# Eight batches through a staged front and six local attention layers: the front's order rewritten around its gathers, gated values in three pieces

## The chip, the cores and the metric

The kernel runs on one core of one Trainium2 chip. The metric is the device time of one execution in microseconds. An execution of the kernel before was also profiled; all rows of traces come from that one.

## The reference

Inputs are eight batches of 256 tokens of 256 numbers, token indices into small tables, and a few condition vectors for each batch. With everything in float32:

```python
# condition block
h = ln(x, pw_g[pathway], pw_b[pathway]); h = ln(h, cp_g[comp], cp_b[comp])
t = ln(x, tm_g[time], tm_b[time]);       s = ln(x, ms_g[scale], ms_b[scale])
m, n, r = (x + mlp_ln(state_k)[:, None, :] for the three condition vectors)
cat = concat([w[0]*h, w[1]*t, w[2]*m, w[3]*n, w[4]*r, w[5]*s])   # w = softmax(aw)
y = mlp_ln(cat)
# 16-head attention on y; its scale comes from maxima and norms of q, k and y
x = x + attention(y)
# modulated linear, attention of each token's 16 heads on one another, modulated linear
o = modulated_linear(heads(modulated_linear(x, cond_512)), cond_512)
# six layers on z, which starts as o; every sublayer first shifts half the features by one token
for i in range(6):
    z = local_attention(shift(z), Wqkv[i], rotary, window=64) @ Wo[i] + z
    a, gate = split(ln(shift(z)) @ W1[i] + b1[i])
    z = (a * gelu(gate)) @ W2[i] + b2[i] + z
out = x + z
```

## The kernel before

`build` (L2240) first lets GpSimd write the identity matrix and zero `state` (128 partitions x 4112 numbers: all eight batches, transposed, each with a column of padding ahead of each half), and then has a barrier of all engines. Three stages follow, each ended by a barrier: `front`, `local_layers` and `write_out`.

**Front** (L153). One batch after another runs through the condition block, the attention in eight pairs of heads, and the attention of each token's heads. Every engine has a list of its own. A helper table says at which step `t` which operation runs for which batch: `for q in batches(t, 60): gather(q)` issues batch q's gather at step 60 + 8q, and where several operations share a step the order of the loops decides. The numbers set nothing but the order within one engine; between the engines semaphores decide. The operations that the steps of the prediction touch:

- SyncE (`sp`) loads inputs at the start: indices, x, the small nets' inputs and first weights (`s_t`, `m_w1`), biases `fcols`, their second weights `m_w2`, the mixer's weights `w_int`, `aff`, and the attention's weights. Twelve of these signal one semaphore, `net`.
- GpSimd (`pool`, L240): `gather` (L263) copies the indices and issues six indirect DMAs (L273), two for each of three tables, into `pw`, `ct` and `ms`. `scale_h`, `scale_t`, `scale_s` and `affine_h` (L282 to L310) multiply by the gathered rows and add them, two instructions each. `net_root` (L255), `dem_root` (L259), `root` (x, h, y) and `scale_root` (L312, writes `scl`) are inverse roots. `head_out` (L324, eight a batch, writes `prodo`) multiplies scores by values of the heads, and `turn_k` writes `kd`.
- TensorE (`pe`): `net_hidden` (L401, its matmuls L405), `net_out` (L413), `style_mm` (L437) and `dem_mm` (L447) for the small nets; `net_flip`, `net_bias` (L430); transposes of x, t, s and h (recorded as L398); `mixer_hidden` (L488); later `scale_row`, whose transposes (L560) bring the score scale into rows.
- ScalarE takes the mixer's hidden values (`hid_t`, L782). VectorE normalises, takes `scol` (L1168) from `scl`, makes the products `prod` (L1237) and the sums `o` of `prodo` (L1267).

Two PSUM banks, `bank_m0` and `bank_m1`, pass between many operations in a fixed cycle (tables `BANK0`, `BANK1`).

**Layers** (L1410). Six layers by eight batches make 48 passes of eight units. A unit projects four heads of q, k or v (`project`, L1598, in high and low halves of the numbers), turns them by the rotary tables, flips them (`flip_qk`: TensorE L1623, ScalarE's copy `qk_t` L1819), scores, softens and flips the probabilities (`prob_t`, L1838), and applies them to the values (`attend`; ScalarE's copy `attn_hi`, L1846). Then come W_o, the layer norm, and W1 in six tiles (NJ = 6), whose second half goes through the GELU. `gelu`, `gate_value`, `hidden_hi` and `hidden_lo` treat the six tiles in two parts of three, and `w_2_mm` waits before tiles 0 and 3. Weights come through one buffer, `w_raw`, in pieces; for the first piece of the first layer (L1517) SyncE issues the load after those of `rot_cos`, `rot_sin`, `band` and two layers' `cols` and `qk_gain`, and VectorE splits it (`split_wqkv`, L1972 and L1974) and then x (L2008, L2010), before TensorE can start.

## Time and profile before

| | |
|---|---|
| median of 3 executions | 3338.82 us (3336.04 to 3339.55) |
| the profiled execution, its own time | 3341.73 us |
| span of its trace | 3340.3 us |
| busy shares: TensorE, VectorE, ScalarE, GpSimd | 92%, 79%, 76%, 62% |
| mean granted clock of TensorE | 0.964 of full speed |
| start to the first batch's hidden values | 0 to 76.6 us |
| batches of the front | 76.6 to 649 us |
| layers | 649 to about 3331 us |

Busy shares are means over stages that differ. The rows below show each engine in short stretches: a timeline row has the start, the duration, the engine and line, output and inputs with their shapes, and in brackets how long the engine was idle before the instruction and which instruction of which engine (or which DMA) ended that.

### The profile page before, as it was taken

The page shows a single profiled execution, that of the slowest core. Times are in us where ns is not written, and L with a number is a line of the kernel's source. Part 1 is how long each engine was busy: PE and PEld are TensorE (multiplying, and loading weights), DVE is VectorE, ACT ScalarE, POOL GpSimd, SP SyncE. Part 2 cuts the span into 40 slices and gives each one's busy share as a digit, 9 for nine tenths or more (in the row PEclk, how much of TensorE's full clock was granted, in tenths as well). Part 3 has the DMA queues.
Part 4 walks back from the last instruction along what each step waited for, and adds up shares of the span by engine and source line. Part 5 has one row for each costly group of instructions (what it writes and reads, how often), then busy time and mean ns, then how long its engine had stood idle before and what let it go on. Part 6 is the DMA issues. An engine that isn't in the chain of part 4 may idle for free. (4 is left out here: it accounts for less than half of the span.)

```text
span 3340.3 us, 80712 instructions
## 1 busy us (share of the span) xinstructions
PE 3079.5 (92%) x29936; PEld 2725.4 (82%) x29936; DVE 2639.1 (79%) x5117; ACT 2535.9 (76%) x7059; POOL 2074.1 (62%) x1536
## 2 busy tenths in 40 slices
PE   3888797279999999999999999999999999999997
PEld 3666565168999899998999989999899998999996
DVE  2368789678888988889887898888888878888884
ACT  0687677168878787878887878878788878888884
POOL 4446654466666666666666667666666666666662
PEclk8898898599999999999999999999999999999999
DMA  3111100010000100001100010000100000100000
GB/s 122 57 36 32 61 7 4 29 41 29 2 2 11 42 30 1 2 2 36 44 3 1 2 36 25 21 2 2 30 23 30 2 2 13 40 29 8 5 8 26
DMA packets 27780, 75.04 MB, mean 22 GB/s; under 512 B 4120, under 2 KB 9848, under 8 KB 27256
## 3 DMA queue, kind: packets, MB, share of 16 engines
q1 hardware_dynamic: 22224, 52.63, 5.0%
q0 software_dynamic: 4864, 16.78, 1.6%
q8 instruction: 242, 3.96, 0.5%
q14 instruction: 146, 1.20, 0.1%
q10 hardware_dynamic: 304, 0.47, 0.1%
HBM read 65.68 MB, written 4.19 MB: 21 GB/s over the span
## 5 line engine op out<-in xcount | busy, mean ns | idle before, releaser
L1571 POOL TENSOR_TENSOR turned<-by_cos,turned 128x512 f32<-128x512 f32 x384 | 493.2, 1284 | 853.6 <-DVE turned L2026 853.5
L1575 POOL TENSOR_TENSOR rnorm<-norm,half 128x8 f32<-128x8 f32 x384 | 788.2, 2053 | 0.0
L1829 ACT ACTIVATE prob<-ps_s,ebias,rnorm 128x128 f32<-128x128 f32 x1536 | 682.0, 457 | 62.5 <-DVE ebias L2047 61.8
L2040 DVE TENSOR_REDUCE negmax<-ps_s 128x8 f32<-128x1024 f32 x192 | 235.1, 1225 | 291.2 <-PE ps_s L1652 290.8
L1838 ACT ACTIVATE prob_t<-ps_t 128x512 f32<-128x512 f32 x384 | 230.0, 599 | 226.6 <-PE ps_t L1661 222.1
L2055 DVE TENSOR_TENSOR prob<-prob,rinv 128x512 f32<-128x512 f32 x384 | 374.9, 976 | 13.1
L1598 PE MATMUL ps_qk<-w_hi,x_hi 128*128 128x512 f32 x768 | 336.9, 439 | 25.1 <-DVE x_lo L2010 14.2
L1737 PE MATMUL ps_f<-hid_hi,w_hi 128*128 128x256 f32 (+1 forms) x1056 | 308.3, 292 | 5.7 <-DVE hid_lo L2101 5.6
L1829 ACT ACTIVATION_READ_ACCUMULATOR prob<-ps_s,ebias,rnorm 128x1 f32 x1536 | 311.6, 203 | 0.0
L1598 PE MATMUL ps_qk<-w_lo,x_hi 128*128 128x512 f32 x768 | 305.2, 397 | 0.0
L1598 PE MATMUL ps_qk<-w_hi,x_lo 128*128 128x512 f32 x768 | 304.9, 397 | 0.0
L2020 DVE TENSOR_TENSOR by_cos<-ps_qk,cos_t 128x512 f32<-128x512 f32 x384 | 265.4, 691 | 44.8 <-ACT sq L1802 42.3
L1737 PE MATMUL ps_f<-hid_hi,w_lo 128*128 128x256 f32 (+1 forms) x1056 | 297.4, 282 | 0.0
L1737 PE MATMUL ps_f<-hid_lo,w_hi 128*128 128x256 f32 (+1 forms) x1056 | 297.2, 281 | 0.0
L1578 POOL TENSOR_TENSOR turned<-turned,rnorm 128x256 f32<-128x256 f32 x384 | 275.6, 718 | 30.1
L1802 ACT ACTIVATE sq<-ps_qk 128x512 f32<-128x512 f32 x384 | 231.0, 601 | 82.6 <-PE ps_qk L1598 78.2
L2026 DVE TENSOR_TENSOR turned<-ps_qk,sin_t 128x256 f32<-128x256 f32 x768 | 286.4, 415 | 0.0
L1819 ACT ACTIVATE qk_t<-ps_t 128x512 f32<-128x512 f32 x384 | 233.3, 608 | 40.9 <-PE ps_t L1623 40.8
L2033 DVE TENSOR_REDUCE sum<-sq 128x8 f32<-128x512 f32 x384 | 259.5, 676 | 0.0
L1623 PE MATMUL ps_t<-ident,turned 128*128 128x128 f32 x1536 | 232.2, 274 | 25.4 <-ACT prob_t L1838 19.7
L1661 PE MATMUL ps_t<-ident,prob 128*128 128x128 f32 x1536 | 242.4, 280 | 1.6 <-DVE prob L2055 1.3
L1693 PE MATMUL ps_f<-attn_hi,wo_hi 128*128 128x256 f32 x768 | 223.0, 290 | 0.8 <-DVE gate L2116 0.4
(289 smaller groups left out, 9690.5 us busy)
## 6 DMA issues: line engine op xcount, KB each, us to landing
w_raw<-in_w_qkv SPq DMA_DIRECT2D x24, 768.0 KB, 4.8
w_raw<-in_w SPq DMA_DIRECT2D x12, 693.0 KB, 4.1
w_raw<-in_w_o SPq DMA_DIRECT2D x12, 512.0 KB, 3.4
w_raw<-in_w SPq DMA_DIRECT2D x6, 768.0 KB, 4.3
x_tok<-in_x SPq DMA_DIRECT2D x8, 256.0 KB
kept<-x_t SPq DMA_DIRECT2D x8, 256.0 KB, 2.0
w_raw<-kept SPq DMA_DIRECT2D x8, 256.0 KB, 3.0
out<-rows_out SPq DMA_DIRECT2D x8, 256.0 KB, 3.0
```

The lines of the kernel that those rows point to most:

```text
L1571: G.tensor_tensor(turned[:, k, :], by_cos[:, :], turned[:, k, :], ALU.add).then_inc(s["turned"], 1)
L1575: G.tensor_tensor(rnorm[:, i % RR, :], norm2[:, k, :], half[:, :], ALU.pow).then_inc(s["rnorm"], 1)
L1578: G.tensor_tensor(kk, kk, rnorm[:, i % RR, GH:].unsqueeze(2).broadcast_to([P, GH, DH]), ALU.mult).then_inc(s["k_unit"], 1)
L1598: last = E.matmul(out, lhs.bitcast(F32R), w[:, kt, g, columns].bitcast(F32R), start=n == 0, stop=n == len(terms) - 1)
L1661: last = E.transpose(ps_t[:, T(h)], prob[:, i % 2, h, :], ident[:, :])
L1737: last = E.matmul(f[0:cut.stop - cut.start, part * N:(part + 1) * N], w[:, kt, cut].bitcast(F32R), x[:, kt, :].bitcast(F32R), start=n == 0 ...
L1829: last = A.activation(prob[:, k, h, :], half_bank(h % 2, k)[:, T(h // 2)], ACT.Exp, bias=ebias[:, i // NU % 2, k, h:h + 1], scale=rnorm[:, ...
L2020: V.tensor_tensor(by_cos[:, :].rearrange("p (a h d) -> p a h d", a=2, h=GH), qk[:, :].rearrange("p (a h d) -> p a h d", a=2, h=GH), cos_t[ ...
L2026: last = V.tensor_tensor(heads(turned[:, k, cut]), heads(qk[:, cut])[:, :, ::-1, :], sn.broadcast_to([P, GH, 2, DH // 2]), ALU.mult)
L2033: V.tensor_reduce(sum2[:, :, 0], sq[:, :].rearrange("p (h d) -> p h d", d=DH), AX.X, ALU.add).then_inc(s["norm2"], 1)
L2040: V.tensor_reduce(negmax[:, k, :, :].rearrange("p u (c o) -> p o u c", o=2), ps_s[:, :, :].rearrange("p o (u c k) -> p o u c k", u=NU, c=2 ...
L2055: V.tensor_tensor(prob[:, k, :, :], prob[:, k, :, :], rinv[:, k, :].unsqueeze(2).broadcast_to([P, GH, P]), ALU.mult).then_inc(s["prob_unit ...
```

## The change

The start: of `state` only the padding columns are zeroed. `m_w2` (now in `w_raw`'s memory) and `aff` have a semaphore of their own, `out`, and are issued before `w_int`; `net_hidden` waits for seven transfers. `style_mm`, `dem_mm`, `dem_root` and what belongs to them stand later, around or in the first batch, and GpSimd's `net_root` stands behind the scalings of batch 0, which now go t, h, s.

The gather has three pieces with waits of their own, at steps 40, 40 and 41, and `scale_root` is at step 56, in front of the gather two batches on (steps 40 + 16). The front's tables are written anew, with 139 steps in place of 161.

```diff
-FRONT_STEPS = 161
-SETUP_SIGNALS = "ids aw rows net int qkv by_pool by_dve by_act by_pe"
+FRONT_STEPS = 139
+SETUP_SIGNALS = "ids aw rows net out int qkv by_pool by_dve by_act by_pe"
...
-        load("net", "m_w20", "m_w21", "m_w22")
-        load("int", "w_int1")
-        load("int", "w_int2")
-        load("net", "aff0", "aff1")
+        load("out", "m_w20", "m_w21", "m_w22", "aff0", "aff1")
+        load("int", "w_int1", "w_int2")
...
+        Y.wait_ge(g["by_pe"], 2)
+        Y.dma_start(w_raw.ap(), io["w_qkv"][0:1, :, :].rearrange("l p (k g n) -> (l p) k g n", k=KT, g=NG)[:, :, 0, :]
+                    ).then_inc(raw_here, 16)
         for b in range(B - 3, B):
             keep(b)
...
-        def gather(a):
-            if a == 0:
-                G.wait_ge(g["ids"], 16)
-            else:
-                G.wait_ge(s["ss"], a)
-                G.wait_ge(s["tt"], a)
-                G.wait_ge(s["hh"], a)
-            done(G.tensor_copy(m["idc"].ap(), m["ids"][:, :, a * NU:(a + 1) * NU]))
-            for k, (dst, tab) in enumerate(((pw, "t_pw"), (ct, "t_ct"), (ms, "t_ms"))):
-                for u in range(NU):
...
+        def gather(a, k):
+            if k == 0:
+                if a:
+                    G.wait_ge(s["h2"], a)
+                    G.wait_ge(s["dma_g"], a * 16 * 3 * NU)
+                else:
+                    G.wait_ge(g["ids"], 16)
+                done(G.tensor_copy(m["idc"].ap(), m["ids"][:, :, a * NU:(a + 1) * NU]))
+            elif a:
+                for reader in (("hh", "tt"), ("ss",))[k - 1]:
+                    G.wait_ge(s[reader], a)
+            dst, tab = ((pw, "t_pw"), (ct, "t_ct"), (ms, "t_ms"))[k]
...
-            E.wait_ge(g["net"], 16 * 12)
+            E.wait_ge(g["net"], 16 * 7)
...
-        nc.gpsimd.memset(state[:, :, :], 0.0).then_inc(begun, 1)
+        nc.gpsimd.memset(state[:, :, ::PAD], 0.0).then_inc(begun, 1)
```

In the layers' setup `band` is issued behind `load_cols(0)`, the first `w_raw` load is gone from there, and VectorE splits it ahead of its waits. Gated values go in three pieces of two tiles:

```diff
+        Y.dma_start(flat(band), io["band"]).then_inc(s["dma_c"], 16)
+        fetch_raw(0)
         load_cols(1)
-        fetch_raw(0)
...
         def hidden_lo(q, part):
-            cut = slice(3 * part, 3 * part + 3)
-            G.wait_ge(s["hid_hi"], 2 * q + part + 1)
+            cut = slice(2 * part, 2 * part + 2)
+            G.wait_ge(s["hid_hi"], 3 * q + part + 1)
...
-                if j % 3 == 0:
-                    E.wait_ge(s["hid_lo"], 2 * q + j // 3 + 1)
+                if j % 2 == 0:
+                    E.wait_ge(s["hid_lo"], 3 * q + j // 2 + 1)
...
         def gelu(q, part):
-            cut = slice(3 * part, 3 * part + 3)
-            A.wait_ge(s["hid_read_act" if part == 0 else "hid_read_dve"], 3 * q + 3)
+            cut = slice(2 * part, 2 * part + 2)
+            if part < 2:
+                A.wait_ge(s["hid_read_act"], 3 * q + 2 + part)
+            if part:
+                A.wait_ge(s["hid_read_dve"], 3 * q + 2 * part - 1)
...
+        split_wqkv(0, 0)
         V.wait_ge(s["lset"], 6)
         V.wait_ge(s["dma_c"], 48)
-        split_wqkv(0, 0)
```

What the tables do to the order is seen at three places. GpSimd at the start of the front, from batch 0's gather on. Before:

```order
14 L273 DMA ms<-in_t_ms,idc 128x512 x2
15 L257 TENSOR_TENSOR m_rs<-m_mv,nhalf 8x3
16 L279 TENSOR_TENSOR xrs<-xmv,nhalf 128x2
17 L261 TENSOR_TENSOR dem<-dem_v,nhalf 128x32
18 L287 TENSOR_TENSOR hh<-xh,pw 128x512
19 L288 TENSOR_TENSOR hh<-hh,pw 128x512
20 L309 TENSOR_TENSOR ss<-xh,ms 128x512
21 L310 TENSOR_TENSOR ss<-ss,ms 128x512
22 L279 TENSOR_TENSOR hrs<-hmv,nhalf 128x2
23 L301 TENSOR_TENSOR tt<-xh,ct 128x512
24 L302 TENSOR_TENSOR tt<-tt,ct 128x512
25 L293 TENSOR_TENSOR hh<-hh,ct 128x512
```

and of the change:

```order
14 L277 DMA ms<-in_t_ms,idc 128x512 x2
15 L282 TENSOR_TENSOR xrs<-xmv,nhalf 128x2
16 L304 TENSOR_TENSOR tt<-xh,ct 128x512
17 L305 TENSOR_TENSOR tt<-tt,ct 128x512
18 L290 TENSOR_TENSOR hh<-xh,pw 128x512
19 L291 TENSOR_TENSOR hh<-hh,pw 128x512
20 L312 TENSOR_TENSOR ss<-xh,ms 128x512
21 L313 TENSOR_TENSOR ss<-ss,ms 128x512
22 L258 TENSOR_TENSOR m_rs<-m_mv,nhalf 8x3
23 L282 TENSOR_TENSOR hrs<-hmv,nhalf 128x2
24 L296 TENSOR_TENSOR hh<-hh,ct 128x512
25 L297 TENSOR_TENSOR hh<-hh,ct 128x512
```

The nets' root `m_rs` moved from the front of the scalings to behind them, and `dem` out of this stretch.

GpSimd around the gather of a middle batch (`scl` is the score scale's root, `prodo` a product of the heads). Before:

```order
116 L270 COPY idc<-ids 128x6
117 L273 DMA pw<-in_t_pw,idc 128x512 x2
118 L273 DMA ct<-in_t_ct,idc 128x1024 x2
119 L273 DMA ms<-in_t_ms,idc 128x512 x2
120 L331 TENSOR_TENSOR prodo<-sc,kd 128x1024
121 L322 COPY kd<-kx 128x512
122 L316 TENSOR_TENSOR scl<-fro,nhalf 16x1
123 L331 TENSOR_TENSOR prodo<-sc,kd 128x1024
124 L279 TENSOR_TENSOR xrs<-xmv,nhalf 128x2
```

and of the change:

```order
117 L334 TENSOR_TENSOR prodo<-sc,kd 128x1024 x2
118 L319 TENSOR_TENSOR scl<-fro,nhalf 16x1
119 L271 COPY idc<-ids 128x6
120 L277 DMA pw<-in_t_pw,idc 128x512 x2
121 L334 TENSOR_TENSOR prodo<-sc,kd 128x1024
122 L277 DMA ct<-in_t_ct,idc 128x1024 x2
123 L334 TENSOR_TENSOR prodo<-sc,kd 128x1024
124 L277 DMA ms<-in_t_ms,idc 128x512 x2
125 L282 TENSOR_TENSOR xrs<-xmv,nhalf 128x2
```

`scl` passed in front of the six issues, and two products stand between them.

ScalarE in a pass of the layers, around the second part's `hid_hi`. Before:

```order
1514 L1838 ACTIVATE prob_t<-ps_t 128x512
1515 L1853 ACTIVATE gate<-hidden 128x512
1516 L1829 ACTIVATE prob,rsum<-ps_s,ebias,rnorm 128x128 x4
1517 L1819 ACTIVATE qk_t<-ps_t 128x4x128
1518 L1846 ACTIVATE attn_hi<-ps_o 128x2x2x128
1519 L1802 ACTIVATE sq<-ps_qk 128x512
```

and of the change:

```order
1526 L1846 ACTIVATE prob_t<-ps_t 128x512
1527 L1861 ACTIVATE gate<-hidden 128x512
1528 L1837 ACTIVATE prob,rsum<-ps_s,ebias,rnorm 128x128 x4
1529 L1854 ACTIVATE attn_hi<-ps_o 128x2x2x128
1530 L1827 ACTIVATE qk_t<-ps_t 128x4x128
```

`attn_hi` and `qk_t` have changed places; the rest of the cycle is as it was.

## Rows read from the trace of the kernel before

**Rows 1.** Windows (us, busy us and count by engine, PEclk, DMA share, GB/s), layers.

```profile
1700.00:2200.00 500.00, 496.10 (x5199) 453.35 (x5198) 419.19 (x835) 406.51 (x1123) 333.24 (x249) 1.00 0.05 15
```

**Rows 2.** Timeline of GpSimd, start: start us, duration us, engine line, [idle before <-releaser].

```profile
0.88 3.53 POOL L2246 MEMSET state<- 128x4112 f32 x1
...
9.03 1.19 POOL L273 DMA_INDIRECT pw<-in_t_pw,idc  x1 [0.65 <-POOL idc L270]
...
40.41 0.89 POOL L257 TENSOR_TENSOR m_rs<-m_mv,nhalf 8x3 f32<-8x3 f32 x1 [23.92 <-DVE m_mv L1025]
...
51.73 1.31 POOL L287 TENSOR_TENSOR hh<-xh,pw 128x512 f32<-128x512 f32 x1
...
63.90 1.07 POOL L273 DMA_INDIRECT pw<-in_t_pw,idc  x1 [0.51 <-POOL idc L270]
```

**Rows 3.** Timeline, start: TensorE, VectorE, ScalarE.

```profile
27.77 2.92 PE L405 MATMUL bank_ob<-s_t,m_w 128*128 128x8 f32 x12 [27.77 <-DMA wide<-in_aff]
...
43.40 0.95 DVE L1034 TENSOR_TENSOR m_out<-m_out,m_rows 8x768 f32<-8x768 f32 x1
...
56.13 5.29 PE L430 MATMUL bank_ob<-m_t,w_int 128*128 128x8 f32 x24 [10.93 <-DVE m_t L1039]
61.27 1.09 PE L398 MATMUL bank_m<-ident,x_tok 128*128 128x128 f32 x4
...
67.31 1.19 PE L488 MATMUL bank_m<-cat,w_mix 128*128 128x256 f32 x2 [0.89 <-ACT cat L773]
...
76.60 0.84 ACT L782 ACTIVATE hid_t<-bank_m,int_bias 128x256 f32<-128x256 f32 x2 [9.54 <-PE bank_m L488]
```

**Rows 4.** Windows, start.

```profile
16.00:28.00 12.00, 0.23 (x1) 0.24 (x2) 0.00 (x0) 0.00 (x0) 0.49 (x1) 1.00 1.00 385
30.00:32.00 2.00, 2.00 (x11) 1.98 (x10) 0.00 (x0) 1.06 (x6) 0.00 (x0) 1.00 0.06 22
74.00:76.00 2.00, 2.00 (x11) 1.77 (x10) 0.00 (x0) 0.00 (x0) 0.00 (x0) 1.00 0.05 18
```

**Rows 5.** Timeline of GpSimd, a batch of the front.

```profile
337.97 1.42 POOL L273 DMA_INDIRECT pw<-in_t_pw,idc  x1 [0.82 <-POOL idc L270]
...
348.94 0.58 POOL L316 TENSOR_TENSOR scl<-fro,nhalf 16x1 f32<-16x1 f32 x1
```

**Rows 6.** Waits from 119 to 649 us: VectorE and TensorE (us, times, longest).

```profile
DVE scol L1168 <- POOL scl L316: 23.1, 7, 8.7
...
PE bank_m L560 <- DVE scol L1171: 19.2, 4, 7.3
```

**Rows 7.** Windows of two batches, hid to hid: with gather, without.

```profile
362.40:429.40 67.00, 55.60 (x348) 41.05 (x344) 51.78 (x86) 48.90 (x144) 42.08 (x29) 0.87 0.13 40
429.40:487.30 57.90, 51.01 (x348) 38.47 (x344) 53.09 (x81) 48.66 (x143) 32.50 (x21) 0.97 0.02 6
```

**Rows 8.** Timeline, front to layers: SyncE, VectorE, TensorE.

```profile
650.24 0.42 SPq L1530 DMA_DIRECT2D band<-in_band  x1
...
657.78 0.96 DVE L1972 CAST w_hi<-w_raw 128x1536 fp32r<-128x1536 f32 x1 [8.10 <-DMA w_raw<-in_w_qkv]
...
661.33 0.69 DVE L2010 TENSOR_TENSOR x_lo<-state,x_hi 128x514 fp32r<-128x514 f32 x1
...
662.28 0.76 PE L1598 MATMUL ps_qk<-w_hi,x_hi 128*128 128x512 f32 x1 [14.22 <-DVE x_lo L2010]
```

**Rows 9.** Groups by line from 760 to 3260 us, ScalarE (busy us, mean ns, idle before).

```profile
L1846 ACT ACTIVATE attn_hi<-ps_o 128x512 fp32r<-128x512 f32 x184 | 111.8, 608 | 0.0
```

**Rows 10.** Waits of TensorE from 760 to 3260 us, the largest.

```profile
PE ps_t L1623 <- ACT prob_t L1838: 13.0, 43, 1.0
```

**Rows 11.** Timeline: the product `prod` beside GpSimd's `prodo`, and without it.

```profile
313.30 2.34 POOL L331 TENSOR_TENSOR prodo<-sc,kd 128x1024 f32<-128x1024 f32 x1
...
313.38 3.08 DVE L1237 TENSOR_TENSOR prod<-kx 128x768 f32<-128x768 f32 x1
...
595.84 0.95 DVE L1237 TENSOR_TENSOR prod<-kx 128x768 f32<-128x768 f32 x1
```

More of the change, by code:

```diff
@@ L150, with front @@
 UN = B * HP
-def front(nc, ctx, io, m, ident, state, kept):
+def front(nc, ctx, io, m, ident, state, kept, w_raw, raw_here):
     g = Signals(nc, ctx, "setup", SETUP_SIGNALS)
@@ L362, in pool @@
[L362 to L377 removed]
+                head_out(q, 1, 0)
@@ L379, in pe @@
+            for q in batches(t, 45):
+                root(q, 'h')
+            for q in batches(t, 80):
+                head_out(q, 1, 3)
+            for _ in once(t, 53):
+                dem_root(_)
     def pe():
@@ new lines, in pe @@
+            for _ in once(t, 42):
+                net_flip(_)
+            for _ in once(t, 46):
+                style_mm(_)
+            for q in batches(t, 46):
+                mixer_hidden(q)
+            for q in batches(t, 44):
+                flip_x(q)
+            for q in batches(t, 45):
+                flip_s(q)
+            for _ in once(t, 0):
+                net_hidden(_)
+            for q in batches(t, 64):
+                project_out(q)
+            for _ in once(t, 50):
+                dem_mm(_)
@@ L1407, with local_layers @@
 RR = 4
-def local_layers(nc, ctx, sems, io, state, kept, ident):
+def local_layers(nc, ctx, s, io, state, kept, ident, w_raw):
     def sb(name, shape, dt=F32):
@@ L1511, in fetch_raw @@
         def fetch_raw(layer):
-            for g in range(NG):
+            for g in range(0 if layer else 1, NG):
                 if g:
```

752 lines of the change are left out of this document (373 added, 379 removed).

## The prediction

> **What bounds the kernel now.** I read the busy shares by stage first. In the middle of the layers TensorE is busy for 496.1 of 500 us at its full 2.4 GHz (granted clock 1.00), while VectorE has 419, ScalarE 407 and GpSimd 333 [rows 1]: there only less work on PE would shorten anything, and an edit to another engine costs nothing until it delays PE by more than the 3.9 us in 500 that it idles. All 48 passes run like this, so some 2670 of the 3340 us are fixed unless PE's own list gets a new wait. What an edit of the order can win lies in four other places: the start before the first batch, the waits between the batches of the front, the step from the front to the layers, and the last pass.
>
> The start comes next, engine by engine [rows 2, 3]. Until 27.77 us PE runs nothing: it waits for `aff`, the last of twelve transfers on one semaphore. Then comes one chain: small nets, their root on GpSimd at 40.41, normalisation, x's own normalisation, GpSimd's scaling of h, s and t from 51.73, the bias at 56.13, flips, the mixer from 67.31, and ScalarE takes its hidden values at 76.60. This moment, hid(0), starts the steady rhythm of the batches, so I measure the start by it. The DMA side stands in the windows: nearly all sixteen engines are busy from 16 to 30, and quiet from 30 [rows 4].
>
> **The change: the start.** GpSimd zeroes 4112 columns of `state` in 3.53 us, now 16 columns; leaving two tenths for these, I take 3.3 us off everything behind the barrier [rows 2]. `aff` and `m_w2` move to a semaphore of their own, so `net_hidden` no longer waits for them, and the nets are done, up to their variance, while the gathers still land. The root of the nets now stands on GpSimd behind the scalings t, h and s, and these need the gathered rows. So the last gather, call its landing G, leads the new chain:
>
> - six scalings of 128x512: 6 x 1.3 [rows 2] = 7.8
> - net root, which was at 40.41: 0.9 [rows 2]
> - nets normalised: 41.30 to 44.35 [rows 2, 3] = 3.1
> - `net_flip` 1.1, priced as four flips [rows 3]
> - flips of x and t, two by 1.1: 2.2
> - `net_bias`: 5.3 [rows 3]
> - flips of s and h: 2.2
> - `style_mm`, 8 matmuls like the 24 that took 5.29: 1.8
> - mixer, from 67.31 to ScalarE's 76.60 [rows 3]: 9.3
>
> That is G + 33.7. For G the trace gives two ends and no row. Below: the second batch's gather, on quiet queues, has its first issue at 63.90 and the queues are quiet at about 74.1 [rows 2, 4], so 10.2 us; with the first issue at 9.03 - 3.3 = 5.7 that makes 15.9. Above: all transfers of the start end at 30, now 30 - 3.3 = 26.7. The bytes of the start other than the gathers compete, but most were asked for later or are bigger, so I take 19, nearer the lower end. Then hid(0) is at 52.7 in place of 76.6: -23.9 (-27.0 to -16.2 over the two ends). The demodulation products (16 small matmuls, again some 2 us) and their flips moved from before the first batch into it, where PE has no reserve yet: +2. Net **-22** (range -14 to -27).
>
> A batch's gathers fetch 256 rows of 2048 numbers of 4 bytes (512, 1024 and 512 from the three tables), 2.1 MB, and the DMA engines were saturated at 385 GB/s while they ran [rows 4]. The Trainium skill, "DMA: Bandwidth & Descriptors", section "Queues, rings and completion order", says that each DMA engine takes turns between the queues it has work for, packet by packet. By that rule the gathers would get half of the 385 GB/s, some 11 us from 5.7, which puts G at about 17 and the sum 1 to 2 us lower; the trace does not show it, since no row tells a gather's landing apart in the crowd.
>
> **The batches.** Seven batches follow the first. Where a gather is still to be issued, the root for the score scale (`scl`) stands behind it: where it came at 348.94, the gather's first issue was at 337.97 [rows 5]; VectorE, waiting with `scol`, lost 23.1 us in seven such waits, PE 19.2 us in four (`L560`) [rows 6]. The period with a gather is 67.0 us, the one without 57.9 [rows 7]. The change puts `scl` ahead of the gather, and cuts the gather in three with products between the pieces. The copy of indices and the six issues (GpSimd is behind them some 8 us) are the same in number; what queues behind them now is `prodo` of the batch before, which VectorE consumes two at a time, and the next batch's x root. The three longest periods, such as the one of 67.0, should come to about 58 to 60: 19.2 us of PE's wait goes, the waits behind it on VectorE (for `inv` and the row maximum) grow by part of that, and a little comes off elsewhere from pieces that start one by one. Together **-20**. Above, nothing is won when the wait moves on to the mixer (-5); below, all periods come down to VectorE's own 53.1 us of work plus gaps (-30). I take the value next to PE's own waiting rows.
>
> **Into the layers.** PE enters them at 662.28 after VectorE's split of the first weights, which begins at 657.78 when 768 KB have landed [rows 8]. The change loads these during the front, in memory that only the small nets used before, and VectorE splits them right behind the barrier that ends the front (649.4), by about 652.4. What is late next is `band`: its issue was at 650.24 [rows 8] and now stands two issues of 0.47 further back, so at 651.2. No row shows its landing: at once is one end, 657.78, when VectorE had the larger weights issued behind it, the other; I take 2.2 us, 653.4. VectorE then copies a last tile, about 0.3, and splits x in two instructions of 0.4 and 0.69, and PE starts 0.3 behind them [rows 8]: 655.0 or so, **-7.2** (-3 to -9). The load itself waits for PE's second signal only and stands on SP's queue behind the last load of x, ahead of the last three stores to `kept`, which nobody waits for until the end of the front.
>
> **In the layers.** Gate, product, high and low part go in three pieces of two tiles in place of two of three. Each engine issues one instruction more per kind and pass: on ScalarE three of 128x512 for two of 128x768, the same elements and one fixed cost more, which is below the 0.61 us of a whole 128x512 one, per kind and pass, on an engine busy for 407 of 500 us [rows 1, 9]. It hides under PE. The first W2 product may begin a piece earlier, but the last piece keeps its place, and it is that which PE's rare waits were for. One swap matters: ScalarE's copy `attn_hi` (0.608 us) [rows 9] now stands ahead of the copy `qk_t`; PE's largest sum of waits in 2500 us is 13.0, for `prob_t`, and I find none for `qk_t` [rows 10], so I cost it at nothing; if its cover went, see the last rival. The end: pieces shorten the last pass by under a microsecond. **0**, give or take 5.
>
> **Sum.** -22 - 20 - 7.2 = -49 from the profiled 3341.73 gives 3292.7; the median of the runs is 2.9 lower, so **3290 us** for the median.
>
> **Rivals.**
>
> *The batches win nothing* (0.21). VectorE's products `prod` took 3.08 us while GpSimd ran `prodo`, against 0.95 alone [rows 11]. If GpSimd's products, freed from behind the gather, fall on VectorE's six or so such products per batch (6 x 2.1 = 12.8 us a batch, twice what a slow period has to gain), the time gained is eaten there: 3290 + 20 = 3310. For it: VectorE is busy 51.8 of 67 us and 53.1 of 57.9 where GpSimd has less [rows 7], close to its limit. Against: this overlap is there already. The Trainium skill, "SBUF — State Buffer", section "SBUF: two separate sides", calls the port that these two engines share an exclusive lock held for a whole instruction against VectorE operations with two SBUF inputs; the 3.08 is in accord with that.
>
> *More goes* (0.13). G at its lower end (-4) and all periods, not only the three, down to VectorE's work (some 3 more in each of seven, -20): 3290 - 24 = 3266.
>
> *ScalarE's copy delays PE* (0.04), the slower side. `attn_hi` ahead of `qk_t` holds PE's scores up in each of the 192 attention groups (184 in the row's stretch). Fully exposed that is 192 x 0.61 = 117 us; the gains of 49 are gone from 49/192 = 0.26 us per group on. At half exposure it gives 3290 + 58 = 3348. For it: PE's order here allows no other work to move up. Against: no wait row names `qk_t`, and ScalarE has 19% to spare.
>
> *Every term at its poor end* (0.03): start -14 (G at 26.7), batches +5 since x's root now stands behind products, entry -3, layers +5: 3338.8 - 7 = 3332.
>
> My forecast has 0.59. A difference of 0.2%, about 6.7 us, is what a measurement of this kernel can tell from none. Faster 0.93, same 0.03, slower 0.04. The range 3266 to 3312 leaves out the last two rivals and the outer parts of the first two, some 0.18.
>
> **What would show it.** In the new profile: `hid_t` of the first batch at 50 to 56 us, released by the mixer, with GpSimd's first scaling starting at about 19; `net_hidden` before 15; `scol` no longer waiting over 1 us for `scl`, and PE's `L560` waits gone; the period of batches 3 to 6 under 61 us; PE's first layer matmul about 7 us behind the state's last write and released by the band load, not by `w_raw`; passes still 55.6 us with PE at 99%. Wrong would be: GpSimd's scaling at 26 or later; batch periods still 64 or more, with `prod` longer; a new row "PE waits for `qk_t`" of tens of microseconds.

## The result, and the profile after

The changed kernel took 3315.47 us (median of 5, 3307.14 to 3324.32) against 3336.04 us for the kernel before (median of 5, 3333.34 to 3339.55). The ratio is 0.9938, with an interval of 0.9917 to 0.9959: faster by 0.6%, where 1.5% were forecast. The time lies 3 us above the top of the range.

The two profiled executions differ more than the medians: 3341.73 us before, the slowest run of its five, and 3307.14 us after, the fastest. I had taken the profile of before as 2.9 us above the median; against five runs it was 5.7, and the profile of the change lies 8.3 below its own median. The changed kernel also spreads over 17 us where the kernel before has 6 in these runs (12 to 18 in the larger groups below). The terms of the sum are therefore read in two profiles of the changed kernel, the first and that of the control below.

**The start.** Timeline of the changed kernel, one row each of the small nets, the gathers, the scalings and the nets' root, then bias, mixer and hidden values:

```profile
9.11 2.92 PE L412 MATMUL bank_ob<-s_t,m_w 128*128 128x8 f32 x12 [9.11 <-DMA fcols<-in_fcols]
...
6.09 1.19 POOL L277 DMA_INDIRECT pw<-in_t_pw,idc  x1 [0.66 <-POOL idc L271]
...
24.82 1.27 POOL L304 TENSOR_TENSOR tt<-xh,ct 128x512 f32<-128x512 f32 x1 [10.51 <-DMA ms<-in_t_ms,idc]
...
32.50 0.86 POOL L258 TENSOR_TENSOR m_rs<-m_mv,nhalf 8x3 f32<-8x3 f32 x1
...
38.95 5.13 PE L438 MATMUL bank_ob<-m_t,w_int 128*128 128x8 f32 x24
...
47.23 3.67 PE L496 MATMUL bank_m<-cat,w_mix 128*128 128x256 f32 x8
...
56.19 0.84 ACT L789 ACTIVATE hid_t<-bank_m,int_bias 128x256 f32<-128x256 f32 x2 [9.68 <-PE bank_m L496]
```

The nets began at 9.11 and no longer wait for `aff`. The first scaling waited 10.51 us for the last gather, which so landed at about 24.8 (G). From there to the hidden values it is 31.4 us. They stand at 56.19, against 76.60 [rows 3]: -20.4 us.

G can also be read from the DMA side, where GpSimd's gathers have a queue of their own (q0, "software"; q1 has SyncE's loads). From 14 to 22 us, when both queues had work, the changed kernel shows (packets, MB, share of the 16 engines):

```profile
q1 hardware_dynamic: 352, 2.02, 60.6%
q0 software_dynamic: 350, 1.28, 39.1%
```

The two queues moved the same number of packets, but the gathers' are smaller there, so they got 1.28 of 3.30 MB. From 8 to 14 us, while the gathers were still being issued, they had less: 166 of 906 packets, 0.55 of 1.98 MB. In the kernel before, the same view from 9 to 28 us holds all of the first gather:

```profile
q0 software_dynamic: 608, 2.10, 32.4%
```

Its last packets are at 27 us; 3.3 us earlier makes 23.9. So the trace of before did tell the gathers apart from the crowd, where I wrote that no row does, and it gave G within 1 us.

The pieces do not let a scaling begin early: in the code every scaling waits for all six transfers of its batch (`dma_g`). In this profile `pw`, all that h's first scaling needs besides x, had landed at 13.9 and `ct` at 21.5 us. What a semaphore for each table would win was not tried.

**The batches.** The best marks are `inv` (ScalarE's inverse row sums, once per batch); the hidden values moved by up to 11 us against it. Timeline of ScalarE in the kernel before, the first and seventh `inv` and the last write of `state`:

```profile
176.19 0.60 ACT L882 ACTIVATE inv<-bank_m 128x512 f32<-128x512 f32 x1 [0.32 <-PE bank_m L615]
...
539.34 0.60 ACT L882 ACTIVATE inv<-bank_m 128x512 f32<-128x512 f32 x1 [0.26 <-PE bank_m L615]
...
648.09 1.02 ACT L908 ACTIVATE state<-bank_m,fcols,dem 128x256 f32<-128x256 f32 x2 [3.87 <-PE bank_m L654]
```

and in the changed kernel:

```profile
155.37 0.61 ACT L889 ACTIVATE inv<-bank_m 128x512 f32<-128x512 f32 x1
...
500.58 0.61 ACT L889 ACTIVATE inv<-bank_m 128x512 f32<-128x512 f32 x1
...
613.41 1.02 ACT L915 ACTIVATE state<-bank_m,fcols,dem 128x256 f32<-128x256 f32 x2 [3.87 <-PE bank_m L661]
```

First `inv` -20.8, seventh -38.8, last write -34.7. The batches thus gave 17.9 us, and the end of the front gave 4.1 of them back. `scol` waited 23.1 us for `scl` in the kernel before, and TensorE 19.2 us behind it [rows 6]. From 119 to 614 us of the changed kernel the first is down to 2.5 us, and the second to 0.9:

```profile
DVE scol L1175 <- POOL scl L319: 2.5, 7, 0.4
```

**The entry to the layers.** Timeline of SyncE, VectorE and TensorE:

```profile
616.49 0.43 SPq L1537 DMA_DIRECT2D band<-in_band  x1
...
616.12 1.76 DVE L1989 TENSOR_TENSOR w_lo<-w_raw,w_hi 128x1536 fp32r<-128x1536 f32 x1
619.97 0.29 DVE L2163 CAST w_hi<-hidden 64x256 fp32r<-64x256 f32 x1 [2.09 <-DMA band<-in_band]
...
621.68 0.77 PE L1606 MATMUL ps_qk<-w_hi,x_hi 128*128 128x512 f32 x1 [8.31 <-DVE x_lo L2025]
```

VectorE splits the weights and then waits 2.09 us for `band`, which it takes up 3.5 us behind the start of its issue. PE starts 8.3 us behind the last write of `state`, where it was 14.2: -5.9 us.

**The layers.** Waits of TensorE from 760 to 3240 us, where [rows 10] had 13.0 for `prob_t` at the head:

```profile
PE ps_qk L1606 <- DVE turned L2041: 18.3, 51, 0.7
PE ps_t L1631 <- ACT prob_t L1846: 9.5, 40, 0.3
PE ps_t L1669 <- DVE prob L2070: 5.3, 6, 1.9
```

`prob_t` is down to 9.5, but there is a new wait of 18.3 us, 51 times, about once a pass: a projection waits for VectorE's rotation to free its PSUM bank. The layer norm's root on GpSimd (`rstd`) marks a pass. In the kernel before:

```profile
1756.36 0.70 POOL L1566 TENSOR_TENSOR rstd<-spread,half 128x2 f32<-128x2 f32 x1
...
1810.43 0.70 POOL L1566 TENSOR_TENSOR rstd<-spread,half 128x2 f32<-128x2 f32 x1
```

and in the changed one:

```profile
1715.52 0.69 POOL L1572 TENSOR_TENSOR rstd<-spread,half 128x2 f32<-128x2 f32 x1
...
1769.84 0.70 POOL L1572 TENSOR_TENSOR rstd<-spread,half 128x2 f32<-128x2 f32 x1
```

54.07 against 54.32 us. From the first to the 46th such root the kernel before took 2446.2 us, the changed one 2455.3: **+9.1 us**, which I had put at 0. (The 55.6 us of a pass in my text was the whole stage over 48, its ends with it.) Two profiles alone could not show so little; the five profiles with the layers of before lie between 2444.8 and 2446.4 (table below), and the five with the layers of the change between 2454.9 and 2456.4.

### The profile page after: what moved, and what is told of

Same layout as the page of the kernel before. It is cut to its first block and busy times, and to the rows that moved or that the text cites. A ratio compares the mean times of both kernels' runs of the same rounds, so it can differ in the third digit from the quotient of the medians.

```text
span 3305.5 us, 81095 instructions
## 1 busy us (share of the span) xinstructions
PE 3076.1 (93%) x29936; PEld 2723.6 (82%) x29936; DVE 2648.3 (80%) x5165; ACT 2546.0 (77%) x7155; POOL 2058.6 (62%) x1584
## 5 line engine op out<-in xcount | busy, mean ns | idle before, releaser
L1581 POOL TENSOR_TENSOR rnorm<-norm,half 128x8 f32<-128x8 f32 x384 | 773.3, 2014 | 0.0
L2070 DVE TENSOR_TENSOR prob<-prob,rinv 128x512 f32<-128x512 f32 x384 | 368.3, 959 | 13.1
L2035 DVE TENSOR_TENSOR by_cos<-ps_qk,cos_t 128x512 f32<-128x512 f32 x384 | 265.1, 690 | 51.6 <-ACT sq L1810 48.8
L1584 POOL TENSOR_TENSOR turned<-turned,rnorm 128x256 f32<-128x256 f32 x384 | 259.6, 676 | 30.1
L334 POOL TENSOR_TENSOR prodo<-sc,kd 128x1024 f32<-128x1024 f32 x64 | 167.2, 2621 | 104.0 <-DVE o L1274 56.5
```

Of the source, the lines that this page charges most:

```text
L1581: G.tensor_tensor(rnorm[:, i % RR, :], norm2[:, k, :], half[:, :], ALU.pow).then_inc(s["rnorm"], 1)
L1584: G.tensor_tensor(kk, kk, rnorm[:, i % RR, GH:].unsqueeze(2).broadcast_to([P, GH, DH]), ALU.mult).then_inc(s["k_unit"], 1)
L2035: V.tensor_tensor(by_cos[:, :].rearrange("p (a h d) -> p a h d", a=2, h=GH), qk[:, :].rearrange("p (a h d) -> p a h d", a=2, h=GH), cos_t[ ...
L2070: V.tensor_tensor(prob[:, k, :, :], prob[:, k, :, :], rinv[:, k, :].unsqueeze(2).broadcast_to([P, GH, P]), ALU.mult).then_inc(s["prob_unit ...
```

## The experiments

All times are medians of the runs with their number; marks (us) come from one profile each. "Front" is the last write of `state`, "46 roots" the time from the first to the 46th `rstd`. Kernels of one group ran on one chip, with its own runs of the kernel before: 3336.04 for the first row, 3344.35 for the next four, 3350.47 for four, 3336.05 for the last four. So ratios compare across groups, times only inside one. The marks of the kernel before are 76.6 for the first hidden values, 176.2 and 539.3 for `inv`, 648.1 for the front and 2446.2 for the 46 roots.

| run | median (runs) | ratio to before, interval | first hidden | 1st, 7th inv | front | 46 roots |
|---|---|---|---|---|---|---|
| the change | 3315.47 (5) | 0.9938, 0.9917 to 0.9959 | 56.2 | 155.4, 500.6 | 613.4 | 2455.3 |
| control | 3317.53 (6) | 0.9914, 0.9898 to 0.9931 | 57.5 | 157.6, 506.8 | 619.4 | 2456.4 |
| gate0_behind | 3313.46 (6) | 0.9910, 0.9893 to 0.9926 | 56.8 | 156.5, 505.7 | 618.2 | 2453.5 |
| layers_old | 3304.39 (6) | 0.9883, 0.9866 to 0.9901 | 55.8 | 155.1, 496.7 | 609.6 | 2446.4 |
| before_sem | 3331.60 (5) | 0.9961, 0.9948 to 0.9975 | 64.8 | 164.8, 528.5 | 637.2 | 2444.8 |
| pieces_kept | 3291.18 (5) | 0.9815, 0.9792 to 0.9839 | 55.6 | 158.0, 513.3 | 626.3 | 2433.7 |
| old_layers_root_first | 3295.27 (5) | 0.9844, 0.9823 to 0.9864 | 52.2 | 154.5, 501.1 | 609.3 | 2445.0 |
| scl_behind | 3355.63 (12) | 1.0024, 1.0012 to 1.0036 | 57.3 | 171.8, 557.5 | 670.1 | 2456.1 |
| one_piece | 3312.76 (6) | 0.9892, 0.9874 to 0.9909 | 56.0 | 155.7, 501.0 | 610.4 | 2454.9 |
| before_scl | 3316.79 (6) | 0.9935, 0.9921 to 0.9950 | 76.1 | 169.4, 511.8 | 620.5 | 2445.7 |
| late_load | 3313.93 (7) | 0.9940, 0.9920 to 0.9960 | 57.3 | 157.2, 498.9 | 611.9 | 2454.9 |
| pe_only | 3309.10 (6) | 0.9921, 0.9900 to 0.9942 | 57.3 | 157.2, 498.9 | 611.9 | 2455.2 |
| best | 3278.55 (5) | 0.9831, 0.9814 to 0.9847 | 52.6 | 152.4, 498.9 | 607.2 | 2434.7 |

The marks of the front need care. Six profiles have exactly the change's front (the change, control, gate0_behind, layers_old, pieces_kept, pe_only), and it ended anywhere from 609.6 to 626.3 us; from first to seventh `inv` it took 341.6 to 355.3. TensorE's granted clock from 100 us to that end goes the same way, from 0.85 to 0.82. And some profiled runs lie off their own median: by -8.3 us for the change, -10.2 for layers_old, -7.4 for one_piece, +6.2 for pieces_kept and +9.5 for scl_behind. A difference of ten us between two single profiles of the front shows nothing by itself.

**control.** No edit.

> The changed kernel again, unchanged, for the spread of its runs (17 us between five of them, where the kernel before had 6) and for a second profile. Theory A: the spread lies in the front, whose end moves by up to 10 us with the clock that TensorE is granted there, while the layers take the same time in every run: here the span from the first projection to the last write-out transposes is 2674.5 us within 1 us, passes 54.32 us. Rival: the layers differ by several us from run to run.

The front ended at 619.4 and not 613.4, and these 6 us were all there at the seventh `inv` (506.8 against 500.6). From the first projection to the first `rstd` it took 114.5, not 111.6. The 46 roots took 1.1 us more, and from the first projection to the write-out it was 2679.3 us against 2674.6, so not within 1. But 9 us of the 10.6 between the two spans lie in the front and the first pass of the layers, where PE has pauses and its granted clock is often down on average (0.97 from 650 to 700 us in the one, 0.93 in the other); the steady layers repeat. The theory held in the main. The front's range of 16.7 us over six profiles is as large as the spread of the runs. In its two extremes TensorE was busy for 402.2 and 416.1 us between 100 us and the front's end, with the same matmuls, so most of the difference is the same work run at the lower clock.

### What costs the layers 9 us

**layers_old**: the layers' tables and two pieces of three, as before, under the changed front.

```diff
-            cut = slice(2 * part, 2 * part + 2)
+            cut = slice(3 * part, 3 * part + 3)
...
-            for q in passes(t, 24):
-                gate_value(q, 2)
...
```

and so on through the four engines' tables, all as in the kernel before.

> The front and the early first weights as changed, the layers' tables and two pieces of three as before. Both theories: passes 54.08 us again, 9 us less over 45 passes. Theory A adds that the first pass loses what it gained by the new tables (the first norm root comes 115.7 us behind the first projection, not 111.6), so the total is 4 to 6 us below the control. Rival: the first pass was shorter for another reason, the front's, and the total is 9 to 10 us below.

The 46 roots took 2446.4 us, 10.0 below the control, and the median fell by 13.1. So the layers' part of the change costs 9 to 10 us here. The first pass did not lose what it had gained (111.6 us to the first root), so it was not the new tables alone that shortened it. The three profiles with the late entry and the old tables have 115.7 to 116.9, and late_load, late with the new tables, 113.9: the rest may be the earlier weights or the clock.

What stands there in a pass? Timeline of VectorE and TensorE in the changed kernel, one place in a pass of the layers:

```profile
1741.54 0.68 DVE L2141 TENSOR_TENSOR gate<-hidden,gate 128x512 f32<-128x512 f32 x1
1742.14 0.47 DVE L2130 TENSOR_SCALAR hidden<-ps_f,cols 42x256 f32<-42x256 f32 x1
...
1743.62 0.49 DVE L2131 TENSOR_SCALAR gate<-ps_f,cols 42x256 f32<-42x256 f32 x1
1744.14 0.69 DVE L2035 TENSOR_TENSOR by_cos<-ps_qk,cos_t 128x512 f32<-128x512 f32 x1
...
1745.64 0.47 PE L1606 MATMUL ps_qk<-w_hi,x_hi 128*128 128x512 f32 x1 [0.34 <-DVE turned L2041]
```

A product of the gate (L2141, 0.68 us) now stands ahead of the reads of the sixth tile (the four of 42 partitions) and of `by_cos`, the rotation's first part. PE needs that rotation done to project the next unit, and waits 0.34 us. In the kernel before, the product stood behind the rotation.

**gate0_behind**: that product behind `rotate`.

```diff
-            for q in passes(t, 23):
-                gate_value(q, 0)
...
             for i in units(t, 1):
                 rotate(i)
+            for q in passes(t, 23):
+                gate_value(q, 0)
```

> The changed kernel with the first of the three products of the gate behind `rotate` on VectorE, not ahead of it. Theory A: the product (0.68 us) ahead of the rotation holds PE's projection once per pass; that wait (18.3 us in 51 times from 760 to 3240 us) goes, passes fall from 54.32 to about 54.1 us, total 8 to 11 us less than the control. Rival B: the passes are longer because three pieces cost ScalarE and VectorE more than two; then passes stay at 54.3 and the total is the control's.

The theory as I had it fell: passes took 54.28 us and the wait for `turned` was still 15.9 us. VectorE and TensorE at the same place show why:

```profile
1746.91 0.47 DVE L2131 TENSOR_SCALAR gate<-ps_f,cols 128x256 f32<-128x256 f32 x1
1747.84 0.48 DVE L2130 TENSOR_SCALAR hidden<-ps_f,cols 42x256 f32<-42x256 f32 x1 [0.46 <-PE ps_f L1745]
...
1751.36 0.47 PE L1606 MATMUL ps_qk<-w_hi,x_hi 128*128 128x512 f32 x1 [0.29 <-DVE turned L2041]
```

With the product gone VectorE arrived 0.46 us early and waited for TensorE's sixth tile. That is a second change of order, one that I had overlooked: PE now computes the scores and flips the probabilities ahead of that tile, where the kernel before computed the tile first. From 760 to 3240 us this new wait is

```profile
DVE hidden L2130 <- PE ps_f L1745: 21.3, 46, 0.5
```

**pe_only** mends only this, on TensorE; **pieces_kept** does both. Edit of pe_only:

```diff
+            for q in passes(t, 22):
+                hidden_mm(q, 5)
             for r in groups(t, 3):
                 score(r)
             for i in units(t, 5):
                 flip_prob(i)
-            for q in passes(t, 22):
-                hidden_mm(q, 5)
```

> The changed kernel with only TensorE's order mended (W1's sixth tile ahead of the probabilities' flip), VectorE's product left ahead of the sixth tile's reads. If the late tile alone made the wait, passes are 53.9 us as in pieces_kept; if the product ahead of the rotation makes it by itself (0.68 us of VectorE's time there), the wait for `turned` stays at 0.2 to 0.35 a pass and passes are 54.1 to 54.3.

> The changed kernel with three pieces kept, the first gate product behind `rotate` on VectorE (as in the run before) and, on TensorE, W1's sixth tile ahead of the flip of the probabilities again, as the kernel before had it. Theory A2 (the order on two engines costs the pass its 0.23 us, not the number of pieces): VectorE no longer waits 0.46 us for the sixth tile, the projection's wait for `turned` goes, passes 54.1 us, 46 passes take 9 us less than in the control, total 8 to 10 us less. Rival B: three pieces cost something of their own; passes stay at 54.25 or above.

pe_only: passes 54.35 us, the wait is still there:

```profile
PE ps_qk L1606 <- DVE turned L2041: 16.6, 51, 0.6
```

pieces_kept: passes 53.87 us, 46 roots in 2433.7, which is 22.7 us below the control's. Its largest waits of PE, 760 to 3240 us:

```profile
PE ps_t L1631 <- ACT prob_t L1846: 10.2, 40, 0.3
PE ps_t L1669 <- DVE prob L2070: 7.5, 7, 2.3
PE ps_qk L1606 <- DVE turned L2041: 2.6, 5, 0.5
```

So neither edit is worth anything alone (0.05 and none per pass), and together 0.46 us in each. The late tile and the product both lay ahead of the same rotation; taking one away leaves the other. In pieces_kept VectorE's wait for the tile (21.3 us above) is gone from the list. Rival B is refuted: with three pieces and the two places mended, a pass is 0.23 us *shorter* than with the layers of before (54.10). The 46 roots of pieces_kept and best take 2433.7 and 2434.7 us, those of every other profile 2444.8 or more. The median is 3291.18, a ratio of 0.9815. How much of that 0.23 is the pieces' and how much the rest of the new tables' I did not part.

### What the start won

**before_sem**: the kernel before with two edits.

```diff
-        load("net", "m_w20", "m_w21", "m_w22")
...
-        load("net", "aff0", "aff1")
+        load("out", "m_w20", "m_w21", "m_w22", "aff0", "aff1")
...
-            E.wait_ge(g["net"], 16 * 12)
+            E.wait_ge(g["net"], 16 * 7)
...
-        nc.gpsimd.memset(state[:, :, :], 0.0).then_inc(begun, 1)
+        nc.gpsimd.memset(state[:, :, ::PAD], 0.0).then_inc(begun, 1)
```

> The kernel before with only two edits: `state` zeroed in its padding columns alone, and `m_w2` and `aff` on a semaphore of their own (net_hidden waits for seven transfers). No table changed. Theory A: the start was held by the wait for `aff` and what queued behind it, and the new order of the start's steps adds little: with gathers landed by about 25 us the scalings start near 25 to 30 and the first hidden values come at 50 to 56 us, against 76.6, total 18 to 24 us below the kernel before. Rival C: the order is what wins, since `dem` (5.5 us on GpSimd) and x's normalisation still stand ahead: first hidden values at 62 or later, total at most 13 below.

First hidden values at 64.84 us, so 11.8 of the 20.4 us, 3.3 of it from the memset; the other 8.6 need the order. GpSimd and ScalarE in its start:

```profile
27.58 0.89 POOL L255 TENSOR_TENSOR m_rs<-m_mv,nhalf 8x3 f32<-8x3 f32 x1 [14.42 <-DVE m_mv L1024]
...
33.77 5.48 POOL L259 TENSOR_TENSOR dem<-dem_v,nhalf 128x32 f32<-128x32 f32 x1
39.16 1.31 POOL L285 TENSOR_TENSOR hh<-xh,pw 128x512 f32<-128x512 f32 x1
...
64.84 0.84 ACT L781 ACTIVATE hid_t<-bank_m,int_bias 128x256 f32<-128x256 f32 x2 [10.36 <-PE bank_m L487]
```

The gathers had landed (at 24.8 in the changed kernel), but GpSimd's first scaling came at 39.16: behind the nets' root, x's root and 5.48 us of `dem`, whose matmuls on PE waited until 28.09 for squares of `k_w` and `o_w`, the last loads. Theory A was wrong and rival C right, in the total too: 12.8 us below the kernel before, ratio 0.9961.

**old_layers_root_first**: on top of layers_old, the root and the normalisation of the nets ahead of the scalings and of h's statistics, since the variance is there at 22.5 us and G is 24.8.

```diff
+            for _ in once(t, 42):
+                net_root(_)
             for q in batches(t, 42):
                 scale_t(q)
...
+            for _ in once(t, 41):
+                net_norm(_)
             for q in batches(t, 41):
                 h_stats(q)
```

> The changed front with the layers of before (as layers_old), and the small nets' root and normalisation ahead of batch 0's scalings on GpSimd and of h's statistics on VectorE. Theory: the nets' variance is there at 22.5 us and the gathers at 24.7, so the root costs nothing there and leaves the chain; the mixer starts behind the flip of h, at 39 to 41 us in place of 47, first hidden values at 48 to 50, total 6 to 8 us below layers_old. Rival: VectorE's normalisation and mixer weights then delay h's normalisation, or the batches behind take the gain back in another wait; hidden values below 51 but total within 2 us of layers_old.

First hidden values at 52.2, so 3.6 earlier than in layers_old and not 6 to 8. VectorE and GpSimd show where the rest went:

```profile
23.72 3.04 DVE L1037 TENSOR_SCALAR m_out<-m_out,m_mv,m_rs 8x256 f32<-8x256 f32 x3 [0.96 <-POOL m_rs L258]
26.80 1.90 DVE L1040 TENSOR_TENSOR m_out<-m_out,m_rows 8x768 f32<-8x768 f32 x1
28.73 1.90 DVE L1041 TENSOR_TENSOR m_out<-m_out,m_rows 8x768 f32<-8x768 f32 x1
...
29.78 1.98 POOL L312 TENSOR_TENSOR ss<-xh,ms 128x512 f32<-128x512 f32 x1
...
52.22 0.84 ACT L789 ACTIVATE hid_t<-bank_m,int_bias 128x256 f32<-128x256 f32 x2 [9.46 <-PE bank_m L496]
```

Beside GpSimd's scalings VectorE's three steps took 3.04, 1.90 and 1.90 us; in the changed kernel they ran without them, at a third to a half:

```profile
33.40 1.04 DVE L1037 TENSOR_SCALAR m_out<-m_out,m_mv,m_rs 8x256 f32<-8x256 f32 x3 [2.14 <-POOL m_rs L258]
34.47 0.95 DVE L1040 TENSOR_TENSOR m_out<-m_out,m_rows 8x768 f32<-8x768 f32 x1
35.45 0.94 DVE L1041 TENSOR_TENSOR m_out<-m_out,m_rows 8x768 f32<-8x768 f32 x1
```

By the marks the 3.6 us were gone at the seventh `inv`, and the front ended at 609.3 against 609.6, which is the rival. But the profile of layers_old is a run 10.2 us below its median, and the one here is on its median (0.3 above), so these marks do not compare like with like. By the ratios of the medians, 0.9844 and 0.9883 with intervals that do not meet, some 13 us were won, which is more than the theory; they come from two chips. Whether the batches keep the start's gain stays open.

### What the batches won

**scl_behind**: the change's order, but the gather in one piece and `scale_root` behind it. **one_piece**: the gather in one piece, `scale_root` left ahead.

```diff
-            for q in batches(t, 56):
-                scale_root(q)
...
             for q in batches(t, 40):
-                gather(q, 0)
+                for k in range(3):
+                    gather(q, k)
+            for q in batches(t, 56):
+                scale_root(q)
```

> The changed kernel with the gather in one piece at its step and `scale_root` behind its six issues, as the kernel before had it. Theory: this is what won the batches' 19 us. `scol` waits 6 to 9 us for `scl` again in three or four batches, PE's L568 waits return with 15 to 20 us, and the time from the first inverse row to the seventh grows by 15 to 20 us over the control. Rival: the batches won by the new order elsewhere (the condition block's steps between the pairs); then under 6 us.

> The changed kernel with the gather in one piece at its step, but `scale_root` ahead of it as changed. Theory: the place of `scl` does it, the three pieces add little; batches within 3 us of the control. Rival: the pieces matter, since products then wait behind 8 us of issues; 5 to 15 us longer than the control.

one_piece: 345.3 us from first to seventh `inv`, against 349.2 in the control and 345.2 in the first profile, and its median, 0.9892 of the kernel before, is not above the control's 0.9914: the three pieces add nothing. (Its end of the front, from the seventh `inv` on, took 109.4 us against 112.5 to 113.0 in the six profiles with the change's front; why I did not follow.) scl_behind: 385.7 us, and the first `inv` 14 us later than the control's. The waits are the ones expected:

```profile
PE bank_m L565 <- DVE scol L1175: 19.0, 4, 7.2
...
DVE scol L1172 <- POOL scl L319: 21.9, 7, 8.3
```

but the price is not. The fair partner is one_piece, which ran on the same chip and differs in the place of `scale_root` alone: the medians are 42.9 us apart, 3355.63 and 3312.76. Windows from first to seventh `inv`, scl_behind and then one_piece:

```profile
171.79:557.47 385.68, 320.32 (x1984) 240.30 (x1984) 288.83 (x470) 281.39 (x839) 205.09 (x135) 0.85 0.10 32
155.74:501.04 345.30, 299.13 (x1984) 224.54 (x1984) 292.87 (x470) 281.14 (x839) 205.93 (x135) 0.93 0.11 35
```

Of the 40.4 us between them 19.2 are idle time of TensorE, as much as the wait's 19.0, and 21.2 are the same 1984 matmuls taking longer, at a granted clock of 0.85 against 0.93. So PE not only waited but also ran its work more slowly. (The profiled run of scl_behind is 9.5 us above its median and that of one_piece 7.4 below, so the size of the second part is of these two runs.) scl_behind is slower than the kernel before, 1.0024: with the rest of the new order, this one root behind the gather costs more than all other parts of the change bring.

**before_scl**: one loop moved in the kernel before.

```diff
-            for q in batches(t, 79):
-                scale_root(q)
...
+            for q in batches(t, 76):
+                scale_root(q)
             for q in batches(t, 60):
                 gather(q)
```

> The kernel before with one edit: `scale_root` stands ahead of the gather two batches on, and nothing else moves. Theory: PE's waits for `scol` (19 to 21 us) go, the time from the first inverse row (inv 0) to the seventh falls from 408 us by 15 to 19, total 14 to 19 us below the kernel before. Rival: scale_root now waits on GpSimd for `fro` with the gather behind it, so the next batch's rows come 4 us later and another wait takes its place; total at most 6 below.

3316.79 us, 19.3 below the kernel before (ratio 0.9935): as much as the whole change in its first measurement (0.9938), less than in the control's (0.9914). First to seventh `inv` took 342.4 us, where the kernel before has 363.2 (the 408 us of the expectation go to the eighth; they fell by the same 20.8). The theory held. PE's wait is down from 19.2 [rows 6] to

```profile
PE bank_m L560 <- DVE scol L1171: 4.5, 2, 2.4
```

### The entry and the best version

**late_load**: the changed kernel with the first weights loaded and split in the layers' start, and that start's loads in the order of before.

```diff
-        Y.wait_ge(g["by_pe"], 2)
-        Y.dma_start(w_raw.ap(), io["w_qkv"][0:1, :, :].rearrange("l p (k g n) -> (l p) k g n", k=KT, g=NG)[:, :, 0, :]
-                    ).then_inc(raw_here, 16)
...
-        split_wqkv(0, 0)
         V.wait_ge(s["lset"], 6)
         V.wait_ge(s["dma_c"], 48)
+        split_wqkv(0, 0)
```

> The changed kernel with the first weights loaded and split in the layers' own start, as before. Theory: PE enters 14.2 us behind the last write of `state` in place of 8.3, total 6 us more than the control (within 3319 to 3326 on the first chips). Rival: the longer pause lowers TensorE's granted clock for longer, so the first pass is longer too (4 us: first norm root 115.7 us behind the first projection in the kernel before, 111.6 to 114.5 with the change); total 9 to 10 us more.

PE starts 14.05 us behind the last write of `state` (611.86) again, with nothing left of the gain:

```profile
625.91 0.77 PE L1602 MATMUL ps_qk<-w_hi,x_hi 128*128 128x512 f32 x1 [14.09 <-DVE x_lo L2021]
```

So the early load is worth 5.5 to 5.8 us; the first root came 113.9 us behind, inside what the two profiles of the changed kernel have (111.6, 114.5), so nothing speaks for the rival. The median (ratio 0.9940) can't show so little beside the spread: the change itself had 0.9938 and 0.9914, and pe_only, on the same chip with the early load, is 4.8 us lower.

**best**: pieces_kept with the edits of old_layers_root_first (`net_root` at step 42 ahead of `scale_t`, `net_norm` ahead of `h_stats`):

```diff
-            for _ in once(t, 45):
+            for _ in once(t, 42):
                 net_root(_)
```

> pieces_kept with the nets' root ahead of batch 0's scalings too. Theory: passes 53.87 us, first hidden values at 52 us in place of 56, total 0 to 4 us below pieces_kept, since the batches behind took most of the start's gain back in old_layers_root_first; about 26 us below the control. Rival: the start's gain is lost wholly and the total is the one of pieces_kept.

3278.55 us, ratio 0.9831 (0.9814 to 0.9847): 57 us below the kernel before, with passes of 53.87 us and the front's end at 607.2. That is the lowest time, but on another chip than pieces_kept, whose ratio is 0.9815 (0.9792 to 0.9839). The two can't be told apart, so the root's new place is not shown to win anything on top, and the rival stands.

## Why the prediction was wrong

| term | forecast | first profile | control's profile |
|---|---|---|---|
| start (first inv) | -22 | -20.8 | -18.6 |
| batches, first to seventh inv | -20, with the front's end | -17.9 | -13.9 |
| end of the front | (in it) | +4.1 | +3.8 |
| entry | -7.2 | -5.9 | -5.6 |
| to the first root | 0 | -4.1 | -1.2 |
| 46 roots | 0 | +9.1 | +10.2 |
| rest | 0 | +0.7 | +1.1 |
| span | -49 | -34.8 | -24.2 |

In the medians the change won 20.6 us; the profiles show more because that of before was 5.7 us above its median and the first of the change 8.3 below. In the control's profile, which lies on its median, the span falls by 24.2 us where 49 were forecast. Of the 25 us that are missing, 10 are the layers, 10 the batches with the end of the front, 3 the start and 2 the entry.

**The step that failed** is "**0**, give or take 5" for the layers. I compared the order of ScalarE there and named `attn_hi` ahead of `qk_t`; the slower rival was built on it, and no wait for `qk_t` appeared. But the layers' tables of all four engines had been rewritten, and that ScalarE's cycle was otherwise "as it was" says nothing of the others. The two moves that mattered were on VectorE (a product ahead of the sixth tile's reads and the rotation) and on TensorE (the probabilities' flip ahead of that tile). I wrote that "the last piece keeps its place" and did not follow the first one. What they cost is shown by pieces_kept, which mends these two places and nothing else and takes 22.7 us off the 46 roots; the rest of the new tables had won some 12 us there, so the whole stood at +9.1 and +10.2. The row that should have warned me is the one I leaned on: with 3.9 us of idle in 500, every third of a microsecond that an engine is late at one place of a pass is paid 48 times. My expected wait in a pass was for the wrong instruction, and the bound of 5 us was no bound: 0.68 us of product by 48 passes is 33.

**The second step** is the base and the end of the front. -20 for the batches was right in mechanism (the stalls of `scol` behind the gather, shown by scl_behind and before_scl) and not far off between the marks, 13.9 and 17.9 in the two profiles and 7.8 to 21.5 in all six. But the end of the front, 4 us longer, was taken at nothing: the last batch's products and sums (`prodo`, `o`) run there without other work beside them, from its `kx` on 51.6 us where it had been 49.3, and `kx` itself comes 1.8 us later behind the seventh `inv`. What makes them longer I did not follow; where the nets' root stands first (old_layers_root_first, best) the whole stretch is 108.3 us, as before.

**The start** was right by luck, by errors that cancelled. G was 24.8, near the upper end of 26.7, and not 19; the DMA view of the kernel before would have given 23.9. The chain behind it took 31.4 and not 33.7, and the +2 for the demodulation did not show before the first `inv`. The turns between queues, which the Trainium skill has in "DMA: Bandwidth & Descriptors", section "Queues, rings and completion order", gave me an estimate of 17 for G. The trace agrees with the turns from 14 to 22 us, where the gathers' queue moved 350 packets and SyncE's 352. But half of the turns was 1.28 MB against 2.02 and not half of the bytes, from 8 to 14 us the gathers had only 166 packets against 740, and G was 7.8 us later than my estimate. Of the three pieces of the gather, to which I gave part of the gain, one_piece shows that they give none.

**The entry** was right to 1.3 us: `band` landed 3.4 us behind the start of its issue, where I had taken 2.2.

**The rivals.** "The batches win nothing" did not happen; its mechanism, stretched `prod`, was there but had been before. "More goes" did not. The measured 3315 is 5 us from the 3310 of the first rival, but by chance: the batches did win, and the loss came from a stage that this rival left alone, the layers. The slower rival had the stage and the kind of event right, at the wrong instruction. And the spread of single runs, 12 to 18 us in the larger groups, belonged in the range: 3.5 us around the median, as the three runs of before had it, was too little to know.

## What to carry to other kernels

In a stage where one engine is 99% busy, list every place of its period at which it needs something from another engine, and read both orders from there back to the last slack: a small instruction moved ahead of such a place can cost up to its own length, once a period (here a product of 0.68 us and a late tile cost 0.46 us together). When one mended place brings nothing, look for the second one under it before giving up the theory; gate0_behind and pe_only each showed nothing, both together 22.7 us. And try the one-line version of a large reordering: here one loop moved (before_scl, 0.9935) was worth about as much as a diff of some 1200 lines (0.9938 and 0.9914).

## What the runs showed of the hardware

- Where TensorE pauses often, a new wait can go with more than its own length: in scl_behind 19.0 us of waits on `scol` came with 40.4 us between the marks of two profiles, at a granted clock of 0.85 in place of 0.93, and with 42.9 us between the medians.
- VectorE's steps with GpSimd at work beside them: 3.04, 1.90 and 1.90 us, against 1.04, 0.95 and 0.94 without it, on 8 partitions. GpSimd's own scaling rose from 1.26 to 1.98. So what is moved into another engine's shadow can lose part of what it saves: these three steps took 3.9 us longer, and the first hidden values came 3.6 us earlier where 6 to 8 were expected. The Trainium skill, "SBUF — State Buffer", section "SBUF: two separate sides", describes the shared port as a lock held for the whole instruction, and these rows agree with one engine being held up by the other.
- 2.1 MB of gathered rows, issued from 6.1 to 13.5 us beside the loads of the start, were complete only at 24.7 us. From 14 to 22 us their queue and SyncE's moved equally many packets (350 and 352), and the gathers' smaller ones carried 39% of the bytes.
